# Cross-attention on one core: the first Q groups ahead of V's last two tiles, and an end turned by row blocks, with one row factor for three rows that VectorE finishes

## What is computed

```python
q, k, v = x @ wq.T + bq, ctx @ wk.T + bk, ctx @ wv.T + bv
scores = einsum('ntd,nsd->nts', heads(q), heads(k)) / sqrt(32) + mask * PAD
ctx = einsum('nts,nsd->ntd', softmax(scores), heads(v))
out = merge(ctx) + x
out = (out - mean(out)) / sqrt(var(out) + 1e-5) * gamma + beta    # per row
```

## Time and profile before

| | us |
|---|---|
| median of 3 runs | 1106.25 |
| the profiled execution | 1106.21 |
| its span, first to last instruction | 1104.4 |
| TensorE busy | 1072.8 |
| VectorE busy | 935.7 |
| GpSimd busy | 775.4 |
| ScalarE busy | 723.0 |

### The profile page before, as it was taken

How to read it: one execution, slowest core, us unless ns; L and a number is a source line. 1 busy time by engine, 2 the same in 40 slices (tenths; PEclk the granted TensorE clock), 3 DMA queues, 4 the chain that set the end, 5 groups by cost and what they waited for, 6 DMA issues and landing times.

```text
span 1104.4 us, 26985 instructions
## 1 busy us (share of the span) xinstructions
PE 1072.8 (97%) x7549; PEld 984.7 (89%) x7549; DVE 935.7 (85%) x1784; ACT 723.0 (65%) x1140; POOL 775.4 (70%) x682
## 2 busy tenths in 40 slices
PE   7999889999999999999999999999999999999985
PEld 7888779999999999999999999999999999999984
DVE  6988578888888888888888888888898888888876
ACT  3321366777777777777777777777777777777653
POOL 4999713676777777777777677777777777777568
PEclk9999999999999999999999999999999999999988
DMA  7754644565565566555556665565666555554452
GB/s 227 256 169 178 206 110 116 135 165 150 148 165 151 156 165 165 152 144 151 142 145 161 164 163 144 150 166 149 158 164 165 146 147 150 143 144 127 127 156 86
DMA packets 176906, 171.34 MB, mean 155 GB/s; under 512 B 110004, under 2 KB 111556, under 8 KB 176868
## 3 DMA queue, kind: packets, MB, share of 16 engines
q1 hardware_dynamic: 167044, 145.36, 46.1%
q10 hardware_dynamic: 9824, 25.50, 10.1%
HBM read 96.76 MB, written 48.85 MB: 132 GB/s over the span
## 4 chain that ended last, share of the span: by engine, by line
PE 91%; DVE 3%; POOL 2%; ACT 1%; issue 1%; DMA 1%; POOLq 0%; ACTq 0%; SPq 0%; DVEq 0%
PE q_ps L863 31%; PE o_ps L935 24%; PE t_ps L897 12%; PE s_ps L883 11%; PE v_ps L608 4%; PE s_ps L886 3%; PE q_ps L567 2%; PE k_ps L567 2%; DVE row_max L1069 1%; POOL k_part L303 1%; POOL y L1154 1%; DMA q_b<-q_b 1%; PE k_ps L624 1%; POOL y L1157 0%; DVE probs L1078 0%
## 5 line engine op out<-in xcount | busy, mean ns | idle before, releaser
L935 PE MATMUL o_ps<-v_tiles,pt 128*128 128x66 f32 x2500 | 309.2, 271 | 0.2 <-DVE attn L989 0.2
L935 PEld LDWEIGHTS o_ps<-v_tiles,pt 128*128 128x128 f32 x2500 | 300.9, 193 | 0.9 <-issue 0.9
L1264 ACT COPY pt<-t_ps 128x512 f32<-128x512 f32 x316 | 184.2, 583 | 157.5 <-PE t_ps L897 154.5
L1069 DVE TENSOR_REDUCE row_max<-s_ps 128x8 f32<-128x616 f32 x256 | 204.7, 800 | 97.3 <-PE s_ps L886 86.1
L1177 POOL TENSOR_TENSOR x_lo<-xT_raw,x_hi 128x512 fp32r<-128x512 f32 x120 | 153.1, 1276 | 188.0 <-ACT x_hi L1236 188.0
L1226 ACT ACTIVATE probs<-probs 128x616 f32<-128x616 f32 x256 | 184.2, 720 | 83.5 <-DVE probs L1078 77.7
L863 PE MATMUL q_ps<-x_lo,wq_hi 128*128 128x512 f32 x496 | 221.9, 447 | 0.0
L1144 POOL TENSOR_TENSOR attn<-attn,x_rows 128x512 f32<-128x512 f32 x124 | 159.1, 1283 | 86.2 <-DVE attn L989 86.2
L1078 DVE TENSOR_TENSOR probs<-s_ps,row_max 128x616 f32<-128x616 f32 x256 | 204.7, 799 | 5.7
L897 PE MATMUL t_ps<-ident,probs 128*128 128x128 f32 x1260 | 193.0, 276 | 4.2 <-ACT pt L1264 2.3
L863 PE MATMUL q_ps<-x_hi,wq_lo 128*128 128x512 f32 x496 | 195.8, 395 | 0.0
(11 more groups left out here) (130 smaller groups left out, 1694.0 us busy)
## 6 DMA issues: line engine op xcount, KB each, us to landing
xT_raw<-in_xT SPq DMA_DIRECT2D x128, 256.0 KB, 3.3
out<-y SPq DMA_DIRECT2D x128, 256.0 KB, 2.8
x_rows<-in_x SPq DMA_DIRECT2D x31, 1024.0 KB, 6.2
k_scratch<-k_out SPq DMA_DIRECT2D x8, 1232.0 KB, 5.1
k_ac<-k_scratch SPq DMA_DIRECT2D x256, 38.5 KB, 5.5
q_a<-q_a ACTq DMA_DIRECT2D x64, 128.0 KB, 3.4
q_c<-q_a ACTq DMA_DIRECT2D x64, 128.0 KB, 3.8
q_b<-q_b ACTq DMA_DIRECT2D x64, 128.0 KB, 4.0
```

Of the source, the lines that this page charges most:

```text
L935: mm = pe.matmul(bank_of(b, t)[:, col:col + tile_cols[i]], pt[h][0:w, i, P * t:P * t + P], v_tiles[v_buffer(b, h)][0:w, i, 0:tile_cols[i]] ...
L1069: dve.tensor_reduce(row_max[:, u, :].rearrange("p (j h) -> p j h", j=2), score_heads(t), AX.X, ALU.max).then_inc(max_ready, 1)
L1264: act.copy(pt[h][0:w, i, :], bank[0:w, :]).then_inc(pt_ready, 1)
```

## The change

**Phase one.** In the last chunk TensorE makes groups 0 and 1 of entry 0's Q after V's third tile (`first_queries`), then V's tiles 3 and 4, then groups 2 and 3. VectorE follows: the low parts of groups 0 and 1 (`first_low`) come before the bias of V's tiles 3 and 4. ScalarE's, GpSimd's and SP's orders stay.

**Blocks 29 to 31.** Normalizing and scaling of blocks 28 and 29 come some steps earlier. The factors of blocks 29 to 31 are made by GpSimd alone (`tail_factors`, now with its tensor_scalar instructions), two columns at a time. SP loads `xT_raw` and V of the last half 1 at the end of the last block's step, after V of half 0 and a store.

**The end.** Half 1 is turned row block by row block, into a tile of its own (`pt_tail`; `tail_turn` on TensorE, `copy_tail` on ScalarE). All products alternate between two banks. ScalarE puts x into banks. VectorE makes no factors; GpSimd makes one power for rows 1 to 3 (`last_factors`), and VectorE finishes these three: `times_gamma` is (row - mean) times gamma, `plus_beta` times the factor plus beta, first three of the one, then three of the other. GpSimd finishes row 0. SP stores row 0 first, then 1 to 3. Its core:

```diff
     def values(c):
         at_least(dve, v_stored, DMA * VT * c)
-        for j in range(VT):
+        for j in range(VT if c < CHUNKS - 1 else 3):
             bias_values(c, j)
             if j < NG:
                 low_keys_out(2 * c * NG + NG + j)
+        if c < CHUNKS - 1:
+            return
+        low_keys_out(2 * c * NG + 2 * NG - 1)
+        for g in range(2):
+            first_low(g)
+        for j in range(3, VT):
+            bias_values(c, j)
     def first_chunk():
...
         for j in range(VT):
+            if (c, j) == (CHUNKS - 1, 3):
+                for g in range(2):
+                    first_queries(g)
...
-    return (q_ps[0], q_ps[1], o_ps, t_ps)[t] if is_last(b) else o_ps
-def last_turn_bank(i):
-    return t_ps if i == 0 else s_ps[(i - 1) // 2][:, (i - 1) % 2, :]
+    return t_ps if is_last(b) and t % 2 == 0 else o_ps
+def tail_turn_bank(t):
+    return (q_ps[0], s_ps[0][:, 0, :], s_ps[1][:, 0, :], q_ps[0])[t]
+def tail_turn_rest(t):
+    return (q_ps[1], s_ps[0][:, 1, :], s_ps[1][:, 1, :], q_ps[1])[t]
 def x_bank(t):
-    return s_ps[1 - t // 2][:, t % 2, :]
+    return s_ps[t // 2][:, t % 2, :]
...
     def store(b, t, par):
-        if is_last(b) and t >= 2:
-            sp.wait_ge(last_ready, t - 1)
+        if is_last(b) and t >= 1:
+            sp.wait_ge(last_ready, t)
         else:
...
                          ).then_inc(x_loaded, DMA)
-        if is_last(a):
-            sp.wait_ge(x_lo_ready, B * KC)
-            sp.dma_start(xT_raw[:], x[LAST].rearrange("(t p) d -> p t d", p=P)
-                         ).then_inc(x_last_loaded, DMA)
-            load_v(a, 1)
         if real(a + 1) and not in_phase_one(a + 1) and not keys_first:
             load_keys(a + 1, 1 - par)
         if real(a - 3):
...
             load_v(a, 0)
         if real(a - 2):
             store(a - 2, 0, par)
+        if is_last(a):
+            sp.wait_ge(x_lo_ready, B * KC)
+            sp.dma_start(xT_raw[:], x[LAST].rearrange("(t p) d -> p t d", p=P)
+                         ).then_inc(x_last_loaded, DMA)
+            load_v(a, 1)
     steps(sp, step)
     for t in range(1, TT):
         store(LAST - 2, t, LAST_PAR)
     for t in range(TT):
         store(LAST - 1, t, 1 - LAST_PAR)
-    for t in (0, 2, 1, 3):
+    for t in range(TT):
...
-        pe.wait_ge(x_last_loaded, DMA)
-        pe.matmul(x_bank(t), ident[:, :], xT_raw[:, t, :], start=True, stop=True).then_inc(x_in_bank, 1)
+    def tail_turn(t):
+        pe.wait_ge(exp_done, LAST * 8 + (5 + t))
+        if t in (1, 2):
+            pe.wait_ge(shifted, LAST * 8 + (6 + t))
+        if t == 3:
+            pe.wait_ge(tail_pt_ready, 2)
+        for i in range(NT):
+            w = tile_rows[i]
...
-        pe.wait_ge(pt_ready, b * (2 * NT) + (NT * h + NT))
+        if is_last(b) and h == 1:
+            pe.wait_ge(tail_pt_ready, 2 * t + 2)
+        else:
+            pe.wait_ge(pt_ready, b * (2 * NT) + (NT * h + NT))
         if v_buffer(b, h) == 2:
             pe.wait_ge(v_loaded[2], DMA * len(pieces))
         else:
             pe.wait_ge(v_loaded[h], (b + 1) * (DMA * len(pieces)))
         if is_last(b):
-            if h == 0 and t == 2:
-                pe.wait_ge(attn_ready, b * 8)
-            if h == 0 and t == 3:
-                pe.wait_ge(pt_ready, b * (2 * NT) + NT + 1)
-            if h == 1:
-                pe.wait_ge(attn_ready, b * 8 + (t + 1))
+            u = 4 * h + t
+            if u > 0:
...
     steps(pe, step)
+    tail_turn(0)
     product(LAST, 0, 0)
+    tail_turn(1)
     product(LAST, 0, 1)
-    for i in range(NT):
-        last_turn(i)
     product(LAST, 0, 2)
     product(LAST, 0, 3)
-    for t in range(TT):
+    tail_turn(2)
+    product(LAST, 1, 0)
+    tail_turn(3)
+    for t in range(1, TT):
         product(LAST, 1, t)
-        x_into_bank(t)
...
-        dve.wait_ge(tail_var, 2 * t + 6)
+    def times_gamma(t):
+        dve.wait_ge(meanvar_done, LAST * 4 + (t + 1))
         dve.wait_ge(gamma_in_bank, 1)
         dve.wait_ge(out_stored[LAST_PAR], DMA * TT * (LAST // 2))
         dve.scalar_tensor_tensor(out=y[LAST_PAR][:, t, :], in0=attn[LAST_PAR][:, t, :],
-                                 scalar=neg_mean[:, t:t + 1], in1=q_ps[0][:, :],
-                                 op0=ALU.add, op1=ALU.mult).then_inc(last_scaled, 1)
+                                 scalar=meanvar[:, t, 0:1], in1=q_ps[0][:, :],
+                                 op0=ALU.subtract, op1=ALU.mult).then_inc(last_scaled, 1)
+    def plus_beta(t):
         dve.wait_ge(beta_in_bank, 1)
-        dve.wait_ge(tail_rstd, t + 3)
-        dve.wait_ge(last_scaled, t - 1)
+        dve.wait_ge(tail_rstd, 6)
+        dve.wait_ge(last_scaled, t)
         dve.scalar_tensor_tensor(out=y[LAST_PAR][:, t, :], in0=y[LAST_PAR][:, t, :],
...
+            if s >= 6 and is_last(a):
+                tail_stats(a - 1, s - 6, 1 - par)
     steps(dve, step)
     read_out(LAST - 1, 1, 3, 1 - LAST_PAR)
+    read_out(LAST, 0, 0, LAST_PAR)
+    read_out(LAST, 0, 1, LAST_PAR)
     tail_stats(LAST - 1, 2, 1 - LAST_PAR)
-    read_out(LAST, 0, 0, LAST_PAR)
+    read_out(LAST, 0, 2, LAST_PAR)
     tail_stats(LAST - 1, 3, 1 - LAST_PAR)
-    tail_factors(LAST - 1, 2, 4)
-    for t in range(1, TT):
-        read_out(LAST, 0, t, LAST_PAR)
+    read_out(LAST, 0, 3, LAST_PAR)
     for t in range(TT):
         read_out(LAST, 1, t, LAST_PAR)
         add_last_row(t)
         tail_stats(LAST, t, LAST_PAR)
-        tail_factors(LAST, t, t + 1)
-        if t >= 2:
-            finish_row(t)
+    for t in range(1, TT):
+        times_gamma(t)
+    for t in range(1, TT):
+        plus_beta(t)
...
-    def tail_factors(lo, hi, n):
+    def tail_factors(b, lo, hi, n):
+        pool.wait_ge(meanvar_done, b * 4 + hi)
+        pool.wait_ge(normed, b * 4 - 4 + hi)
+        pool.tensor_scalar(var_eps[:, lo:hi], meanvar[:, lo:hi, 1], LN_EPS, None, ALU.add
+                           ).then_inc(tail_var, 1)
+        pool.tensor_scalar(neg_mean[:, lo:hi], meanvar[:, lo:hi, 0], -1.0, None, ALU.mult
+                           ).then_inc(tail_var, 1)
...
+    def last_factors():
+        pool.wait_ge(meanvar_done, LAST * 4 + TT)
+        pool.wait_ge(normed, LAST * 4)
+        pool.tensor_scalar(var_eps[:, 1:TT], meanvar[:, 1:TT, 1], LN_EPS, None, ALU.add
+                           ).then_inc(tail_var, 1)
+        pool.wait_ge(tail_var, 11)
+        pool.tensor_tensor(rstd[:, 1:TT], var_eps[:, 1:TT], minus_half[:, 1:TT], ALU.pow
+                           ).then_inc(tail_rstd, 1)
...
-                if 3 <= s < 7:
-                    scale_rows(a - 2, s - 3, par)
+                if s == 0:
+                    scale_rows(a - 3, 3, 1 - par)
+                if s == 2:
+                    tail_factors(a - 2, 2, 4, 2)
+                if 2 <= s < 6:
+                    scale_rows(a - 2, s - 2, par)
+            elif is_last(a + 1):
+                if s >= 4:
+                    scale_rows(a - 2, s - 4, par) if s < 7 else tail_factors(a - 1, 0, 2, 1)
             elif s in (5, 7) and real(a - 2):
...
     steps(pool, step)
-    tail_factors(0, 2, 1)
     add_rows(LAST - 1, 3, 1 - LAST_PAR)
+    tail_factors(LAST - 1, 0, 2, 3)
     scale_rows(LAST - 1, 0, 1 - LAST_PAR)
-    tail_factors(2, 4, 2)
-    for t in range(1, TT):
-        scale_rows(LAST - 1, t, 1 - LAST_PAR)
-    for t in range(3):
-        tail_factors(t, t + 1, t + 3)
+    tail_factors(LAST - 1, 2, 4, 4)
+    scale_rows(LAST - 1, 1, 1 - LAST_PAR)
+    scale_rows(LAST - 1, 2, 1 - LAST_PAR)
+    tail_factors(LAST, 0, 1, 5)
+    scale_rows(LAST - 1, 3, 1 - LAST_PAR)
+    last_factors()
     scale_rows(LAST, 0, LAST_PAR)
-    tail_factors(3, 4, 6)
-    scale_rows(LAST, 1, LAST_PAR)
...
+    def copy_tail(t):
+        act.wait_ge(tail_turned, t + 1)
+        act.copy(pt_tail[:, 0:NT - 1, P * t:P * t + P],
+                 tail_turn_bank(t).rearrange("p (i q) -> p i q", q=P)).then_inc(tail_pt_ready, 1)
+        w = tile_rows[NT - 1]
+        act.copy(pt_tail[0:w, NT - 1, P * t:P * t + P], tail_turn_rest(t)[0:w, 0:P]
+                 ).then_inc(tail_pt_ready, 1)
+    def x_into_bank(t):
+        act.wait_ge(x_last_loaded, DMA)
+        act.wait_ge(tail_pt_ready, 2 * (t // 2) + 4)
+        act.copy(x_bank(t), xT_raw[:, t, :]).then_inc(x_in_bank, 1)
...
+            if is_last(a) and 2 <= s < 6:
+                norm(a - 2, s - 2, par)
...
     steps(act, step)
+    copy_tail(0)
     exponent(LAST, 1, 3)
+    copy_tail(1)
     norm(LAST - 1, 0, 1 - LAST_PAR)
-    copy_pt(LAST, 1, 0)
-    copy_pt(LAST, 1, 1)
+    x_into_bank(0)
+    x_into_bank(1)
+    copy_tail(2)
+    copy_tail(3)
     norm(LAST - 1, 1, 1 - LAST_PAR)
-    for i in range(2, NT):
-        copy_pt(LAST, 1, i)
+    x_into_bank(2)
+    x_into_bank(3)
     norm(LAST - 1, 2, 1 - LAST_PAR)
     norm(LAST - 1, 3, 1 - LAST_PAR)
     act.wait_ge(scale_loaded, 2 * DMA)
-    act.wait_ge(attn_ready, LAST * 8 + 5)
+    act.wait_ge(tail_pt_ready, 2 * TT)
```

(49 more changed lines are left out.)

41 lines of the change are left out of this document (14 added, 27 removed).

## The result

The changed kernel took 1099.29 us (median of 5, 1097.81 to 1100.64) where the kernel before, beside it, took 1105.67 (5, 1104.24 to 1106.25): ratio 0.9942, 95% interval 0.9931 to 0.9953, 6.4 us less. A later series of the same two kernels gave 1098.61 (n 6) against 1105.28 (n 11), ratio 0.9948 (0.9934 to 0.9961). The forecast was 1096.5 with a range of 1093.5 to 1102.5, so direction and range hold and 2.8 us of the gain are missing. The profiled execution took 1099.97, its span is 1097.7; before they were 1106.21 and 1104.4.

The account below looks back on a forecast made before the run. TensorE, busy 97%, bounds the middle; the ends are bound by a transfer, a transfer and the clock, and GpSimd's queue. Terms sum to 9.8 us won: 1106.2 - 9.8 = 1096.4, given as 1096.5, range 1093.5 to 1102.5.

Parts of the forecast that it names:

- start, as it arrives: End of phase one: first scores at 133.5 instead of 136.10, 2.6 us won, 2.5 carried through the middle.
- block 30's normalization: Block 30's step 4: a normalization put in front of an exponent delays one transposition, 0.3 us lost.
- step 7's product: Last block, half 1: this product ends at 1070.2 instead of near 1076.6, 6.4 us won.
- last addition after it: The end: the last addition starts 2.0 us after step 7's product instead of 3.2, 1.2 us won.
- GpSimd's queue: The end: GpSimd's remaining operations take 20.5 us instead of 21.4, 0.9 us won.
- stores behind it: Very end: row 0 is stored first and three more stores queue behind it, 0.44 us each; 0.9 us lost.
- rival 3: Start gives nothing, because V's last store, now later, holds the barrier: 1099 us, chance 0.13.
- The second hole: Last block's step 4 (half 1's first scores), 3.15 us idle awaiting `q_moved[1]`: start 1059.4 instead of 1062.68, at full clock.
- Rival 1: Last block: `q_moved[1]` still takes over 8 us beside three early stores; 6.4 us come back, 1102.5 us, chance 0.12.
- Rival 4: From step 4 to the end: the clock, once down, never comes back; 15 us slower, 1111 us, chance 0.04.
- GpSimd's small operations: The end: small tensor_scalars on GpSimd taken at 0.2 us each, seven on the path, at most 9 us more.
- rival 2: The end waits for dear small GpSimd operations, half-way to 1.51 us each (4.6 us): 1101 us, chance 0.11.

Follow-up runs that it names:

- e4: The changed kernel with SyncE's wait for V's last store moved behind the barrier, ahead of the first V load; 1099.92 us, ratio 0.9957 to the kernel before.
- e8: The changed kernel with block 28's three stores issued, in the last block, behind half 0's V loads and block 29's store; 1097.58 us, ratio 0.9939.
- e5: The changed kernel with the last block's four stores issued in the order 1, 2, 3, 0; 1097.39 us, ratio 0.9938 to the kernel before.
- e1: The kernel before with only phase one's new order of V and Q; 1103.32 us, ratio 0.9982.

## Why the prediction was right, and where 2.8 us went

In terms of the first trace, microseconds won at each step. Block 31's scores are 0.26 ahead; with the 0.24 lost in block 30 added back, the start gave 0.5:

| step | predicted | first trace |
|---|---|---|
| start, as it arrives | 2.5 | 0.5 |
| block 30's normalization | -0.3 | -0.24 |
| step 7's product | 6.4 | 6.3 |
| last addition after it | 1.2 | 1.5 |
| GpSimd's queue | 0.9 | 0.1 |
| stores behind it | -0.9 | -1.4 |
| sum | 9.8 | 6.8 |

- **Start: the term that failed.** The prediction put the barrier at 133.3, "just behind VectorE's last Q instruction", and the first scores at 133.5, with a lower bound of 1.5 won should V's last store land 1 us late. Without the wait for that store the kernels show 133.85 and 2.57 us won on average: the mechanism and its size were right. The store costs 0.76 of it on average, 0.8 was won in the first trace (below the bound), 1.8 over six. VectorE's last Q instruction, forecast 0.5 earlier, ended at 133.42 against 133.44 in the first trace, and 0.3 earlier on average. "I carry 2.5 us through the middle" failed too: 1.6 arrive on average, and the slow stretch in block 0 takes 0.2 to 0.6 where it occurs. The prediction saw that GpSimd's product, the V store and the x loads would all move 0.7 us later (the product moved by 1.2). It named the store as what could hold the barrier, in its lower bound and in rival 3, but put it at nothing in the sum. In the first trace the barrier opened at 135.0, 1.6 behind VectorE's end, where e4 has 0.3: so 1.3 us are the store's there. Rival 3 happened in part.
- **The second hole.** Gone, as forecast, with the clock at 1.00. Step 4 came at 1059.89, 0.26 ahead in all, against 1059.4: q_b landed in 6.2 us, not 5.1 to 5.7. The row that gave 5.1 had no three stores queued right ahead. Step 7's product was met all the same within 0.1, since VectorE's steps took a little less than assumed. Rival 1 held in this milder form. e8's trace gives its price, 1.1 us at the end. Rival 4 is not seen in any trace with the new loads.
- **GpSimd's small operations.** 0.22 us each, 0.2 taken; rival 2 is out. What was missed is the 0.08 between most operations and the next. With 0.3 from start to start, the four operations of a factor group took 1.6, 1.6 and 1.4 us instead of 1.4, 1.4 and 1.2, while the forecast wait of 0.3 for row 1's normalization did not come. The queue took 21.3 us (1071.79 to 1093.08), not 20.5. So the hand-over of factor work ate the row that was saved: 21.4 before.
- **VectorE** ended 0.4 ahead of GpSimd, 0.3 forecast, and 1.2 us of the end by medians (1.8 by the trace of e5) lay in the order of the stores: rows 1 to 3 stood ready while row 0 was awaited. The loss was seen (0.9) and undersized (1.4).
- **Single trace against medians.** By medians the start is worth 1.9 and the end 4.1, by the first trace 0.5 and 6.3; the forecast was 2.5 and 7.3. (In e1's trace 0.7 of the gain came at step 4's wait, which the new loads shorten anyway.) So the total came out nearer than its larger part, and the end is the larger miss: the forecast priced it from one execution of the kernel before. The 21 executions of the kernel before beside e1 to e4 differ: twelve have a mean granted clock of 0.990, as in that trace, and took 1104.9 to 1106.2; of the nine above it, eight took 1103.3 to 1104.8. Why the end gives 4.1 and not 6.3 is not shown further.

## To carry to other kernels

When work ahead of a barrier is reordered, list for every engine the last thing it waits for before the barrier, transfers on the way out included: the new order is only as early as the latest of them. A small move that the next step needs should have no large transfers issued just ahead of it on any queue; stores that nobody awaits can go behind. And where several engines finish rows together, give the last row to the engine that waits, and store in the order in which rows get ready.

## Not expected of the hardware

- The same 128 KB move within SBUF landed in 8.1 to 8.7 us with 1 MB, a second 1 MB and twelve small loads issued on the other queue from 4 us ahead of it, in 6.0 to 6.9 with 1 MB and three stores of 256 KB, and in 3.6 to 4.2 with 1 MB alone.
- The same 2.45 us of idle TensorE in block 0 were followed by about 3.4 us at a granted clock of 0.50 in six traces and by 1.00 in four, with the same order of work.
- GpSimd's power over 128 rows: 0.58, 0.71, 0.89 and 1.04 us for 1, 2, 3 and 4 columns; its tensor_scalar 0.22 to 0.24 for any of these widths. A further row in a common factor costs about 0.15 us.
- Executions of one kernel on one chip differ by up to 6.5 us, which is the whole effect studied. With the stores out of the way the spread was 0.9 and 1.2 us, in only five executions each.
